# First attention: values products and turned scores of a step taken ahead of the other scores products on TensorE

## The reference, cut to what matters

```python
def _L0_attn_ref(x, Wq, Wk, Wv, Wo):        # x (4, 512, 256), 16 heads of 16
    q = split_heads(x @ Wq.T)
    k = split_heads(x @ Wk.T)
    v = split_heads(x @ Wv.T)
    sim = jnp.einsum('bhsd,bhtd->bhst', q, k) * scale
    causal = jnp.tril(jnp.ones((S, S), dtype=bool))
    sim = jnp.where(causal[None, None], sim, -jnp.inf)
    weights = jax.nn.softmax(sim, axis=-1)
    out = jnp.einsum('bhst,bhtd->bhsd', weights, v)
    return out.transpose(0, 2, 1, 3).reshape(B, S, D_MODEL) @ Wo.T
x = x + _layernorm(_L0_attn_ref(_layernorm(x), Wq, Wk, Wv, Wo))
```

## Time and profile before

| what | value |
|---|---|
| median of three runs | 1222.49 us (1221.7 to 1225.82) |
| the profiled execution | 1221.95 us, its span 1220.2 us |
| TensorE busy | 1160.6 us (95% of the span) |
| VectorE / ScalarE / GpSimd busy | 846.3 / 799.6 / 580.7 us |
| TensorE, first attention: first least turn to last | 57.26 to 223.47 us |
| chain that ended last, by engine | PE 76%, DVE 8%, ACT 6%, issue 4%, POOL 3% |

### The profile page before, as it was taken

One profiled execution on the slowest core, in us unless ns is written; L12 is line 12 of the kernel. 1 busy time (PEld: TensorE's weight loads), 2 busy tenths in 40 slices (PEclk: granted clock), 3 DMA queues, 4 the chain that ended last, 5 costly groups with the idle time before them and its releaser, 6 DMA issues.

```text
span 1220.2 us, 25017 instructions
## 1 busy us (share of the span) xinstructions
PE 1160.6 (95%) x7868; PEld 988.4 (81%) x7868; DVE 846.3 (69%) x2663; ACT 799.6 (66%) x2069; POOL 580.7 (48%) x844
## 2 busy tenths in 40 slices
PE   6999999899999999999999999999998879999986
PEld 5766566689999989999989999889986769999962
DVE  5778888576677667876677876668865755555535
ACT  3587888677778776778776787777786524444422
POOL 4063655454334444457343466334453446666650
PEclk9999999999999999999999999999999989999998
DMA  8965555256631211213121131211114237777766
GB/s 271 284 190 168 173 175 170 89 176 191 189 114 57 91 51 57 81 53 123 35 69 37 35 109 67 69 36 54 64 54 132 78 112 116 118 119 118 119 110 223
DMA packets 111779, 139.58 MB, mean 114 GB/s; under 512 B 11364, under 2 KB 94820, under 8 KB 111524
## 3 DMA queue, kind: packets, MB, share of 16 engines
q1 hardware_dynamic: 97204, 119.10, 32.2%
q0 software_dynamic: 14448, 18.88, 9.5%
HBM read 63.36 MB, written 61.87 MB: 103 GB/s over the span
## 4 chain that ended last, share of the span: by engine, by line
PE 76%; DVE 8%; ACT 6%; issue 4%; POOL 3%; DMA 2%; SPq 1%; POOLq 0%; ACTq 0%; DVEq 0%
PE bank L1500 56%; PE bank L1742 5%; PE bank L1926 5%; PE bank L1561 2%; DVE bank L1127 2%; PE bank L1597 2%; PE bank L1614 2%; POOL xs_rows L684 1%; PE bank L1604 1%; PE bank L1905 1%; PE bank L1936 1%; ACT pT L842 1%; POOL sum_rows L746 1%; ACT p L966 1%; DVE hs L1358 1%
## 5 line engine op out<-in xcount | busy, mean ns | idle before, releaser
L1127 DVE CUSTOM_DVE_ANT_0 bank<-bank,mask 128x512 f32<-128x512 f32 (+3 forms) x512 | 235.1, 522 | 42.3 <-PE bank L1500 21.6
L957 ACT ACTIVATE p<-bank,stat 128x512 f32<-128x512 f32 (+3 forms) x256 | 131.6, 527 | 127.0 <-DVE stat L1127 127.0
L537 POOL CAST w_hl<-raw_qkv 128x512 fp32r<-128x512 f32 x96 | 58.8, 613 | 301.9 <-DMA raw_qkv<-in_qkvo 154.2
L1500 PE MATMUL bank<-xT,w_hl 128*128 128x512 f32 x768 | 190.3, 396 | 0.0
L1500 PEld LDWEIGHTS bank<-xT,w_hl 128*128 128x128 f32 x768 | 142.2, 188 | 37.1 <-issue 2.0
L746 POOL DMA_INDIRECT sum_rows<-mid,goal x79 | 122.9, 1555 | 70.7 <-DVE mid L1464 68.1
L966 ACT ACTIVATE p<-p,stat 128x512 f32<-128x512 f32 (+3 forms) x256 | 123.1, 553 | 14.7 <-DVE stat L1361 14.7
L538 POOL TENSOR_TENSOR w_hl<-raw_qkv,w_hl 128x512 fp32r<-128x512 f32 x96 | 124.2, 1294 | 7.8
L1383 DVE TENSOR_TENSOR o<-bank,o 128x512 fp32r<-128x512 f32 x64 | 44.2, 690 | 109.4 <-ACT o L973 109.4
L1500 PE MATMUL bank<-pT,v 128*128 128x256 f32 (+2 forms) x576 | 117.1, 348 | 0.0
L1500 PE MATMUL bank<-k,q 128*128 128x512 f32 (+2 forms) x576 | 111.5, 337 | 2.5 <-ACT pT L950 1.7
(11 more groups left out here) (248 smaller groups left out, 2561.3 us busy)
## 6 DMA issues: line engine op xcount, KB each, us to landing
raw_qkv<-in_qkvo SPq DMA_DIRECT2D x32, 768.0 KB, 5.3
xs_rows<-blank SPq DMA_DIRECT2D x32, 520.0 KB, 3.3
xs_rows<-blank SPq DMA_DIRECT2D x5, 2730.0 KB, 14.6
xrow<-xs_rows SPq DMA_DIRECT2D x79, 130.0 KB, 2.5
raw_o<-in_qkvo SPq DMA_DIRECT2D x32, 256.0 KB, 3.6
sum_rows<-blank SPq DMA_DIRECT2D x3, 2176.0 KB, 8.5
stk<-xT SPq DMA_DIRECT2D x96, 64.0 KB
stk<-k_hl SPq DMA_DIRECT2D x96, 64.0 KB
```

The costliest lines, as they stand in the source:

```text
L537: link(pool.tensor_copy(hi, raw))
L957: act.activation(p2[:, n % 2, POFF[qi]:POFF[qi + 1]], s2(t), ACT.Exp, scale=-1.0, bias=stat2[:, 0, n % 2, t:t + 1], accum_out=stat2[:, 1, ...
L1127: return dve.tensor_tensor_reduce(scores, scores, mask[:, TB - scores.shape[1]:], scale=-1.0, scalar=-2.0 * MASKED, op0=ALU.add, op1=ALU.m ...
L1500: ins = pe.matmul(out, a, b, start=start and i == 0, stop=stop and i == len(pairs) - 1, **kw)
```

## The change

Three pieces of TensorE's step are put in another order; no product, wait or tile is added or taken away, and the other engines' programs stay as they are. "Values one" moves behind the sum turn, the first half of the projection and the turn of `xn_mid`. "Other values" follows it at once. "First turned" comes next, and "other scores" last of the four.

```diff
-                if 1 <= s <= N1:
-                    ...
-                    values(s - 1, TPB)
 
                 if s >= 3 and s % 2 == 1:
...
+                if 1 <= s <= N1:
+                    if s % 2 == 1 and s >= 3:
+                        pe.wait_ge(a1_oe, s // 2)
+                    pe.wait_ge(a1_vpad, s)
+                    pe.wait_ge(a1_sel, 4 * (s - 1) + 1)
+                    values(s - 1, TPB)
+                    pe.wait_ge(a1_sel, 4 * s)
+                    for n in range(TPB - 1, 0, -1):
+                        ins = values(s - 1, n)
+                    ins.then_inc(a1_pv, 1)
+                if 0 <= s < N1:
+                    pe.wait_ge(a1_m, 2 * (s + 1))
+                    for i, (a, n) in enumerate(S1_PARTS):
+                        if s >= 1 and i:
+                            pe.wait_ge(a1_exp, 5 * (s - 1) + i + 3)
+                        score_t(a, n).then_inc(a1_st, 1)
                 if r < N1:
                     for a, n in S1_REST:
...
                     score(r, 1, 2).then_inc(a1_s, 1)
-                if 0 <= s < N1:
-                    ...
-                        score_t(a, n).then_inc(a1_st, 1)
-                if 1 <= s <= N1:
-                    pe.wait_ge(a1_sel, 4 * s)
-                    for n in range(TPB - 1, 0, -1):
-                        ins = values(s - 1, n)
-                    ins.then_inc(a1_pv, 1)
```

## The result

The changed kernel takes 1248.65 us, the median of four runs (1247.82 to 1249.55), against 1222.1 us of the kernel before in the same comparison: ratio 1.0215, with a 95% interval of 1.0187 to 1.0242. It is 26.5 us slower. The forecast was 1242.2 us, the range 1232 to 1253. The profiled execution of the changed kernel took 1248.15 us, its span 1246.4 us.

The account below looks back on a forecast made before the run. It took ScalarE's round to bound even steps before the change and VectorE's round to set steps after. 17.3 us over 29 steps, 2.0 for steps 0 and 1 and 0.4 behind step 31 gave 1242.2 us, range 1232 to 1253.

Parts of the forecast that it names:

- What lets a step end: Next least turn waits for ScalarE in even steps, VectorE's round having 0.54 us slack; in step 7, odd, none.
- First turned: TensorE's start after the least turn: +1.94 us in even steps as before; +2.52 instead of +2.09 in odd steps.
- Other scores: Even steps start them at +2.48 us instead of +1.15; steps become 5.38 us even and 5.96 us odd.
- Projection steps: Steps 10, 18 and 26: taken as 8.0 us each, the projection's second half starting at +4.70 or slipping slightly.
- The term taken as nothing: In odd steps, other values might wait slightly for GpSimd's fourth clearing; the wait vanishes as steps lengthen, so nothing added.
- The sum over the 29 steps: From the turn beginning step 2 to that beginning step 31: 155.87 us before, 173.2 after, +17.3 us.
- steps 0 and 1: Start of the stage, partly at half TensorE clock: 2 us more for both together, bounds 1 and 4.
- what follows step 31: Nothing waits for other scores there, but step 31's first turned lose the odd steps' 0.43 us: 0.4 us added.
- Rival (a), the clock: Idle time lowers TensorE's clock in a quarter of 30 steps, +3 us each: 24 us more, about 1266 us; chance 0.10.
- (b): Only ScalarE's round counts, so only odd steps lose, 0.43 us each: about 1230 us; chance 0.06.
- (c): TensorE's queue is the bound; values products fill the 2.6 us wait for row copies: 1219.9 us; chance 0.04.
- (d): SyncE's load queue sets the pace and hides a slower TensorE: about 1224 us; chance 0.03.

Follow-up runs that it names:

- run 6: Changed kernel with two of VectorE's five second maxima left out in each step, for timing only: 1223.16 us, ratio 1.0023 to the kernel before.
- run 7: Kernel before with two of VectorE's five second maxima left out in each step: 1217.55 us, ratio 0.9986.
- Run 3: Kernel before with only the sum turn, first projection half and turn of xn_mid moved ahead of values one: 1220.32 us, ratio 0.9991.
- run 2: Kernel before with values one and other values together behind the sum turn, other scores still ahead of first turned: 1228.98 us, ratio 1.0067.
- run 1: Kernel before with only first turned moved ahead of other scores, values products where they were: 1234.58 us, ratio 1.0103.
- run 4: Changed kernel with product (1,3) of the other turned computed four times instead of once, filling TensorE's idle time: 1235.07 us, ratio 1.0131.
- run 8: Kernel before with SyncE's queue clearing half as many rows per step of the first attention: 1220.68 us, ratio 1.0000.

## Why the prediction held, and where its sizes were off

The sign and the range were right, and so was the mechanism of the forecast; but that mechanism makes about 9 of the 21.7 us in the 29 steps. The rest is the clock, which the forecast did not have. The middle was 6.5 us low. That it came so near is in part luck, since a term sized too large and one left out nearly cancel.

- **What lets a step end.** Right. The slack of 0.54 us that VectorE's round had in even steps, and its lack in odd ones, is what runs 6 and 7 show: cutting 0.5 us there gives nothing in even steps and 0.5 us in odd ones such as 3 and 7 before, and 0.5 us in most plain steps of both kinds after. "Odd" is too wide, though: steps 5 and 9 did not gain before.
- **First turned.** +1.94 in even steps, as worked out. In odd steps they start earlier than the +2.52 of the sum: in step 21 at +2.24 (189.74 to 191.98, below).
- **Other scores: the term that was mis-sized.** The sum put them 0.54 us behind the start of the first turned, which was the distance from first turned to other values in the earlier trace rows. They follow at 0.34 us: 208.51 to 208.85 above. Together with the tighter packing of transposes and values products in odd steps, the step came out at 5.21 and 5.52 us where 5.38 and 5.96 were forecast. This is step 21 in TensorE's timeline of the changed kernel:

```profile
189.74 0.65 PE L1561 MATMUL bank<-ident,least 128*128 128x128 f32 x4
190.23 0.60 PE L1561 MATMUL bank<-ident,o_sum 128*128 128x128 f32 x4
190.76 1.29 PE L1614 MATMUL bank<-pT,v_pad 128*32 128x256 f32 x28
191.98 0.61 PE L1604 MATMUL bank<-stk 64*128 64x512 f32 x3
192.32 0.56 PE L1597 MATMUL bank<-stk 64*128 64x384 f32 x5
```

  From turn to other scores it is 2.58 us; the sum had 3.06. I had added up starts between different neighbours, and neighbours of one kind follow each other sooner: least turn to sum turn 0.49 here, least turn to values one 0.58 or 0.59 in the earlier trace rows. The tail was right: 2.37 in the sum, 2.39 measured, and the 0.53 ahead of it was 0.54.
- **Projection steps.** 8.0 us forecast, 7.54 measured, less than the 7.87 of before. Step 10 has the second half of the projection at 124.15 - 119.77 = +4.38, not +4.70: the extras ahead of values one help here. Run 3 shows this part alone (7.68).
- **The term taken as nothing,** other values waiting for GpSimd's fourth clearing: in the changed kernel weight loads of values products waited for GpSimd 2.7 us in seven times, and no product did. In run 2, with shorter steps, they waited 10.0 us in 25 times, and the products 1.7 us.
- **The sum over the 29 steps** was +17.3 forecast, about +9 at full clock, +21.7 with the clock. The terms around it were small: steps 0 and 1 cost 2.86 us (2.0 forecast, 1 to 4 as bounds), what follows step 31 1.4 (0.4 forecast).
- **Rival (a), the clock,** had a chance of 0.10 and was priced at +24 us as an alternative. It came true beside the forecast: ten falls in the stage, 13 us in the 29 steps and part of the 2.86 of the first two. Nine steps were touched, near the quarter that it assumed, but each lost about 1.3 to 1.6 us and not 3. The step that failed is the one that held it unlikely because the clock stayed up behind 246.1 to 249.5, and with it the sign "a granted clock of 1.00 from about 66 us on". Nor was TensorE only 80% busy: in step 24 it was busy for 4.76 of 5.21 us, with modelled ends. One stretch that passes at 50% busy does not show that a pattern repeated thirty times will.
- **Rivals (b), (c), (d)** did not hold. (b), that only ScalarE's round counts, is excluded by runs 1, 2 and 6. (c), TensorE as the bound, by runs 4 and 6: 0.5 us more of products costs nothing in a plain step at full clock, two maxima less give 0.5. (d), the load queue, holds single steps (run 8), and the changed kernel had no wait for a load at all. The "three waits, 2.3 us" of the earlier trace rows in the prediction count one wait twice, at the weight load and at its product; there were two waits, 1.4 us at the weight loads.

The Trainium skill (page "TensorE: Matmul & The Clock Gate", What's actually happening) says that activity releases the throttle. Run 4 agrees: with more work in the wait, 10.2 us of low clock against 41.

## What to carry to other kernels

An in-order engine that feeds two others has two rounds per step, one through each; find the slack of both before moving work, and measure it where each of them sets the end. Moving work into one engine's wait pays only if nothing that another engine waits for stands behind it: here 0.8 us of values products and 0.3 us of turned scores filled a wait of 2.6 us in the whole stage and pushed VectorE's input back by 1.1 us in each even and 0.8 us in each odd plain step. Where a change adds idle time to TensorE in a repeated pattern, add a price for the clock to the forecast instead of keeping it as a rare rival.

## What the runs showed of the hardware that I had not expected

More idle time did not mean a lower clock. Even steps take 5.21 us in the changed kernel and 5.22 in run 1, with the same products, and in run 1 TensorE is busy for less of one (4.33 us of step 4 against 4.76 of the changed kernel's, with modelled ends). Yet behind the start of the stage the granted clock fell nine times in the changed kernel and not once in run 1 in their profiles, and over the whole kernel it was 0.974 to 0.978 against 0.985 to 0.988 in all four executions of each. One difference is where the idle time lies: run 1 has 0.81 us of it ahead of the first turned in step 6 and the rest behind the other scores, the changed kernel all of it behind the other scores. Another is that odd plain steps are longer in the changed kernel (5.52 us against 5.21 to 5.40 in steps 3 to 9 and 17). Which of them decides was not tested and stays open. With 0.5 us of repeated products in that place (run 4) one fall was left behind the start.

Two products of TensorE that follow each other started 0.34 us apart or 0.54 us apart by what the second one was (other scores or values products), although the first group was the same three products. Distances between starts belong to the pair, not to the first of them. By their rows the scores and turned scores read 64 partitions and the values products 128; whether that is the reason was not tested.
